# Sum of squares in a gated RMS norm: halves added before the product, one product in place of two

## What is computed

```python
y = (y_intra + y_inter).reshape(B, H, L, D).transpose(0, 2, 1, 3)
rms = jnp.sqrt(jnp.mean(jnp.square(y), axis=-1, keepdims=True) + RMS_EPS)
y = y / rms * gnorm_w
gate = (hidden_states @ Wg.T).reshape(B, L, H, D)
y = y * (gate * jax.nn.sigmoid(gate))
return y.reshape(B, L, H * D) @ Wo.T
```

## Time and profile before

| | us |
|---|---|
| median of 3 runs | 1121.64 |
| lowest, highest | 1119.6, 1122.24 |
| the profiled execution's own time | 1125.82 |
| its span in the trace (first to last instruction) | 1124.0 |
| PE busy in it | 1078.1 (96%) |
| DVE, ACT, POOL busy | 768.3, 550.6, 206.4 |

### The profile page before, as it was taken

How to read it: one execution, slowest core, us unless ns; L and a number is a source line. 1 busy time by engine, 2 the same in 40 slices (tenths; PEclk the granted TensorE clock), 3 DMA queues, 4 the chain that set the end, 5 groups by cost and what they waited for, 6 DMA issues and landing times. The chain is left out here.

```text
span 1124.0 us, 14213 instructions
## 1 busy us (share of the span) xinstructions
PE 1078.1 (96%) x4680; PEld 808.6 (72%) x4680; DVE 768.3 (68%) x1492; ACT 550.6 (49%) x1133; POOL 206.4 (18%) x131
## 2 busy tenths in 40 slices
PE   5869999999999999999999999999999969999898
PEld 1747777777777777777777777777776448888676
DVE  5777876877788678868877887778676785444411
ACT  2445555666555566555666555666555434222300
POOL 2412121211222121122111221211121530000000
PEclk8989999999999999999999999999999989999999
DMA  6111311220131013102201310131030431111011
GB/s 221 48 52 56 121 38 37 83 77 19 37 112 37 19 37 112 37 27 82 95 19 37 103 46 19 37 112 37 19 106 22 192 130 40 56 37 57 29 38 37
DMA packets 37464, 70.89 MB, mean 63 GB/s; under 512 B 2936, under 2 KB 19576, under 8 KB 35520
## 3 DMA queue, kind: packets, MB, share of 16 engines
q1 hardware_dynamic: 36720, 70.16, 19.3%
q10 hardware_dynamic: 720, 0.43, 0.1%
HBM read 68.33 MB, written 2.24 MB: 63 GB/s over the span
## 5 line engine op out<-in xcount | busy, mean ns | idle before, releaser
L1299 POOL TENSOR_TENSOR q_sin<-q_sin,cst 128x512 f32<-128x512 f32 x64 | 83.0, 1296 | 395.8 <-ACT q_sin L751 395.8
L1292 POOL TENSOR_TENSOR dec<-dec,future 128x1024 f32<-128x1024 f32 x31 | 80.3, 2591 | 273.8 <-ACT expg L770 273.8
L54 PE MATMUL ps_gt<-hT_hi,wg_hi 128*128 128x512 f32 x256 | 126.4, 494 | 3.6 <-DVE sg L986 3.6
L848 ACT ACTIVATE work<-ps_y 128x512 f32<-128x512 f32 x64 | 38.3, 598 | 186.1 <-PE ps_y L673 185.3
L54 PE MATMUL ps_q<-hT_hi,wq_hi 128*128 128x512 f32 x256 | 126.5, 494 | 2.8 <-DVE q_cos L966 2.3
L54 PE MATMUL ps_o<-wo_hi,z_hi 128*128 128x512 f32 x260 | 104.1, 400 | 2.4 <-DVE z_lo L49 2.4
L56 PE MATMUL ps_o<-wo_hi,z_lo 128*128 128x512 f32 x260 | 103.1, 396 | 0.0
L55 PE MATMUL ps_o<-wo_lo,z_hi 128*128 128x512 f32 x260 | 102.7, 395 | 0.0
L55 PE MATMUL ps_gt<-hT_lo,wg_hi 128*128 128x512 f32 x256 | 101.9, 398 | 0.0
L56 PE MATMUL ps_q<-hT_hi,wq_lo 128*128 128x512 f32 x256 | 101.9, 398 | 0.0
L56 PE MATMUL ps_gt<-hT_hi,wg_lo 128*128 128x512 f32 x256 | 101.8, 398 | 0.0
(11 more groups left out here) (239 smaller groups left out, 2537.9 us busy)
## 6 DMA issues: line engine op xcount, KB each, us to landing
dec<-gT_dram SPq DMA_DIRECT2D x32, 512.0 KB, 5.4
raw_q<-wq_in SPq DMA_DIRECT2D x32, 256.0 KB, 2.6
raw_g<-wg_in SPq DMA_DIRECT2D x32, 256.0 KB, 2.9
raw_o<-wo_in SPq DMA_DIRECT2D x8, 1024.0 KB, 7.0
raw_pair<-wkv_in SPq DMA_DIRECT2D x8, 512.0 KB, 4.6
raw_pair<-wgu_in SPq DMA_DIRECT2D x6, 512.0 KB, 3.3
raw_gu<-wgu_in SPq DMA_DIRECT2D x5, 512.0 KB, 3.3
qT<-wmod_in SPq DMA_DIRECT2D x2, 1024.0 KB, 7.0
```

What stands on the lines that cost most here:

```text
L54: pe.matmul(out, w_hi, x_hi, start=first, stop=False)
L848: nc.scalar.activation(sq, ps_y[:], ACT.Square).then_inc(sq_done, 1)
L1292: nc.gpsimd.tensor_tensor(cells, cells, future[:].unsqueeze(1).broadcast_to([P, GRP * CPB, CHUNK]), ALU.add).then_inc(mask_done, 1)
L1299: nc.gpsimd.tensor_tensor(q2, q2, sinT, ALU.mult).then_inc(qsin_done, 1)
```

## The change

`y^2` is a sum over 128 partitions, so the upper 64 can be added to the lower 64 first. ACT now writes the squares of partitions 0 to 63 into `sq[0:64]` and those of 64 to 127 into a new tile `sq_top`, both float32. DVE adds them into `sq_sum` (64 x 512). ACT rounds `sq_sum` into partitions 0 to 63 of `sq_parts` (`round_squares`, new), and DVE writes the rest into partitions 64 to 127 of it. One product of ones with `sq_parts` then sums high and low halves together. On PE the whole of `g_block` (12 products) stands ahead of it.

```diff
             def square_sum(g, t):
 
                 pe.wait_ge(sqhi_done, g * 8 + (t + 1))
-                nc.tensor.matmul(ps_ss[:], ones[:], sq_hi[:], start=True, stop=False)
                 pe.wait_ge(sqlo_done, g * 8 + (t + 1))
-                nc.tensor.matmul(ps_ss[:], ones[:], sq_lo[:], start=False, stop=True)\
+                nc.tensor.matmul(ps_ss[:], ones[:], sq_parts[:], start=True, stop=True)\
                     .then_inc(ss_ready, 1)
...
                 if project:
-                    g_block(g, t, 0, KT - 1)
+                    g_block(g, t, 0, KT)
                 square_sum(g, t)
-                if project:
-                    g_block(g, t, KT - 1, KT)
...
+            def round_squares(g, t):
+                act.wait_ge(sqsum_done, g * 8 + (t + 1))
+                nc.scalar.activation(sq_parts[0:64], sq_sum[:], ACT.Copy).then_inc(sqhi_done, 1)
...
-                nc.scalar.activation(sq, ps_y[:], ACT.Square).then_inc(sq_done, 1)
-                nc.scalar.activation(sq_hi[:], ps_y[:], ACT.Square).then_inc(sqhi_done, 1)
+                nc.scalar.activation(sq[0:64], ps_y[0:64], ACT.Square)
+                nc.scalar.activation(sq_top[:], ps_y[64:128], ACT.Square).then_inc(sq_done, 1)
...
                 if c == 1:
                     copy_kT(g, b)
+                round_squares(g, t)
                 decays(g, t + 1)
...
-                dve.wait_ge(sqhi_done, g * 8 + (t + 1))
-                split_lo(nc.vector, sq_lo[:], sq, sq_hi[:]).then_inc(sqlo_done, 1)
-                dve.wait_ge(sqlo_done, g * 8 + (t + 1))
+                dve.wait_ge(sq_done, g * 8 + (t + 1))
+                nc.vector.tensor_tensor(sq_sum[:], sq[0:64], sq_top[:], ALU.add).then_inc(sqsum_done, 1)
+                dve.wait_ge(sqsum_done, g * 8 + (t + 1))
                 dve.wait_ge(sg_done, g * 8 + (4 * half + 4))
                 nc.vector.tensor_tensor(z[:], ps_y[:].rearrange("p (h i) -> p h i", h=GRP),
                                         sg[:, half, :, rows_of(t)], ALU.mult).then_inc(zz_done, 1)
+                dve.wait_ge(sqhi_done, g * 8 + (t + 1))
+                split_lo(nc.vector, sq_parts[64:128], sq_sum[:], sq_parts[0:64]).then_inc(sqlo_done, 1)
```

More of the change, by code:

```diff
@@ L231, in block_attention @@
         sq = work[:].rearrange("p h i -> p (h i)")
-        sq_hi, sq_lo = sb("sq_hi", [P, HALF], F32R), sb("sq_lo", [P, HALF], F32R)
+        sq_parts = sb("sq_parts", [P, HALF], F32R)
+        sq_top, sq_sum = sb("sq_top", [P // 2, HALF]), sb("sq_sum", [P // 2, HALF])
+        win_lo = sb("win_lo", [P, KT, P], F32R)
         rms = sb("rms", [P, HALF])
@@ L249, in block_attention @@
         silu_c = sb("silu_c", [P, KT * B])
-        win, win_hi, win_lo = (w[:].rearrange("p (k h) -> p k h", k=KT) for w in (q_cos, sq_hi, sq_lo))
+        win, win_hi = (w[:].rearrange("p (k h) -> p k h", k=KT) for w in (q_cos, sq_parts))
         rows = cross[:, 1, 0:2 * H].rearrange("p (r h) -> p r h", r=2)
@@ L329, in block_attention @@
         sq_done = sem("sq_done")
+        sqsum_done = sem("sqsum_done")
         sqhi_done = sem("sqhi_done")
@@ L1108, in _ @@
                     dve.wait_ge(win_split, 1)
-                    split_lo(nc.vector, win_lo, win, win_hi).then_inc(win_split, 1)
+                    split_lo(nc.vector, win_lo[:], win, win_hi).then_inc(win_split, 1)
             dve.wait_ge(tables_loaded, 16)
```

## The result

The changed kernel takes 1176.12 us in the median of 4 runs (1174.0 to 1176.79), the kernel before 1121.94 (1119.6 to 1123.52). The ratio is 1.0475, 95% interval 1.0456 to 1.0493: slower by 54 us. The prediction was 1165, range 1146 to 1178: the direction and the mechanism held, and the size was 11 us short, a fifth of the loss. The result lies only 2 us under the top of the range.

A forecast was written before the change was run, and what follows sets the result against it. The prediction took PE, saturated in the loop, as the bound. A stall in every step, net of the removed product, gave +39 us and the tail +4: 1121.64 + 43 = 1165 us, range 1146 to 1178.

The forecast's parts named there:

- The bound: In the loop, PE limits the time: busy for all 750.00 us between 100 and 850 us.
- The other signs: PE's busy share falls about 6%; line 690 waits about 60 times, 40 to 50 us; DVE's sum takes 0.69 us.
- Part 1: On PE, one product of squares less saves 0.23 us a step, 14 us in 60 steps.
- Part 2: On PE, three gate products move ahead without added work, giving the chain from `ps_y` 2.62 us to make `sq_parts`.
- Part 3: Chain on ACT and DVE: low half late, PE idle 0.78 us, step +0.66 us net, +39 us in 60 steps.
- the rule that says so: On DVE, an instruction starting in another partition group waits for earlier ones: up to 0.05 us a step, 3 us in all.
- The restart: On PE after a wait, the next product comes 0.34 us later instead of 0.23, with 0.23 as low bound.
- the high end of the range: 0.70 us a step, 10 us in the tail and a few for the cover: 1177 us.
- Part 4: Work behind the waits: exponentials just fit and cost nothing; `z_lo` keeps 0.64 of 1.34 us of cover.
- Part 5: Tail, steps 4 to 7 of the last group without gate products in front: +4 us, bounds 1 and 10.
- the chain is hidden, whole or half: Two rivals on the chain to `sq_parts`: fully hidden, about 1112 us; half hidden, 1117 to 1124; chance 0.04 each.
- The third rival: Cover of `z_lo` at the out product or of the exponentials on ACT breaks too: 15 us more, 1180; chance 0.08.

The follow-up runs named there:

- the order of PE alone: Kernel before with the whole gate block moved ahead of its two products of squares, nothing else touched: 1123.74 us, ratio 1.0003.
- the changed kernel with one wait: Changed kernel without PE's wait for the high half ahead of the product of squares: 1170.09 us, ratio 1.0422 to the kernel before.
- The kernel with `z` behind: Changed kernel with `z` computed behind the low half on DVE instead of ahead of it: 1180.48 us, ratio 1.0501 to the kernel before.

## Why the prediction was right, and what it missed

- **The bound** was PE, without any slack in the loop, and the changed kernel shows 44 us of idle PE in the same stretch. Right. The other signs that were named are there too: PE waits at line 690 for the low half 64 times and 49.5 us in all.
- **Part 1, the product that goes: 14 us.** Right in size when it is tried alone with cover behind the gate block (13.2 us in the loop). In its old place it gave 5.
- **Part 2, the order costs nothing.** Right, 1.0003.
- **Part 3, the chain.** Up to the start of the rounding every entry is within 0.01 us of the trace: the squares 0.60 apart, half height no cheaper, the sum at 1.23. Then two terms were too small. The low half starts 0.04 later than I had it; `z` is in front of it, and it does not overlap `z`. I had the rule that says so and left it out of the sum. And the hand-over to PE was taken as 0.05 from the earlier trace rows, where the product has one wait; line 690 has two, and it took 0.14. The restart was 0.31, not 0.34. Together the step is 0.75 us longer (15.26 us the even one, 12.16 the odd one), not 0.65. In 60 steps that is 6 of the 11 us missed. It is also more than the 0.70 that the high end of the range allowed.
- **What the prediction did not look at: the end of the loop's pass.** In step 7 the next scores start 0.59 us behind the product, not 0.31:

```profile
299.50 0.46 PE L690 MATMUL ps_ss<-sq_parts,ones_r 128*128 128x512 f32 x1 [0.73 <-DVE sq_parts L49]
300.09 1.12 PE L662 MATMUL ps_s<-qT,kT 128*128 128x512 f32 x2
```

  Step 7 is 0.38 us longer by it than the other odd steps, in the six passes that another follows; the last is 0.13 longer; 2.5 us in all. The trace shows the loop's jump (line 391) in PE's sequencer between the two products:

```profile
L391 PEldq ALU_OP  x1: 32/32/32, 299.5 to 299.5; - x1
L391 PEldq COMPARE_BRANCH  x1: 213/213/213, 299.6 to 299.6; - x1
L391 PEldq FUSED_REGOPS  x1: 50/50/50, 299.9 to 299.9; - x1
```

  With the order of PE alone, two products of squares are the last of the pass as well, but PE does not stop in front of them. There the same jump (line 388) lies at 494.7 to 495.2, the scores start at 495.92 in full stride, and step 7 takes 11.43 us like the other odd steps. So here the jump costs nothing while PE still has products to work on, and is paid when it comes behind a wait.
- **Part 4, the cover.** Right. The logarithm starts 0.26 us behind the end of the exponentials (339.71 to 339.97), so they cost nothing, and in the loop PE never waits for `z_lo` (the one wait of 2.4 us behind the last step is in both traces): in odd steps it is ready 7.73 us after `ps_y`, and its reader starts at 8.36, 0.63 of cover against 0.64 predicted. The reader that was missing in this part, the out product's other operand `wo_lo`, does not bind in the changed kernel, since the stall in even steps moves PE back as well. It binds as soon as the stall is mended.
- **Part 5, the tail: +4.** It was +7.5, of which 0.75 belongs to the 60th step. Step 4 gave 0.85 against 0.7 predicted, step 5 gave 0.72 against 1.3, step 6 alone 3.3 against 1.3. (Step 5 was long before already, 14.88 us with the subtraction of 1.81 us; in the profiles of the five other kernels with that tail it takes 13.8 to 14.0, so that against them it is some 1.6 longer.) What comes behind the last `ps_y` is 1.9 longer, where 0.4 was predicted and the product comes 0.64 later; in the six profiles whose tail has no added halves this stretch lies between 223.4 and 226.3 us (226.3 changed), so the rest of it shows nothing. Step 6: its product starts at 941.60, 1.8 us later than before after `ps_y`, half a microsecond more than I had. The rest is the clock. PE had nothing to do from 939.3 to 941.6, and from 942.8 on the granted clock was at the lower of its two levels, 1.2 GHz. By stretch (first number of the pair behind the busy times is the clock), and two rows of the out product in it:

```profile
942.80:946.20 3.40, 3.40 (x10) 2.62 (x9) 1.46 (x5) 0.63 (x2) 0.00 (x0) 0.52 0.00 0
```

```profile
942.61 0.39 PE L54 MATMUL ps_o<-wo_hi,z_hi 128*128 128x512 f32 x1
...
943.60 0.63 PE L54 MATMUL ps_o<-wo_hi,z_hi 128*128 128x512 f32 x1
944.03 0.63 PE L55 MATMUL ps_o<-wo_lo,z_hi 128*128 128x512 f32 x1
```

  Products there are 0.43 apart instead of 0.23, and the seven that fell into it make some 1.4 us. In the profile of the changed kernel with one wait, which differs in the tail by that wait alone, PE stands idle just as long, but the clock stays at 1.00 and step 6 took 8.96 us and not 10.50. The kernel with `z` behind has the dip too. So that part is one that a run may have or not.
- **The rivals.** That the chain is hidden, whole or half, failed on the point named: half height buys nothing (0.685 us for 64 partitions of the sum). The third rival, a cover that breaks besides, is not what added the 11 us. That the measured time lies in the range owes something to luck: its high end was made of 10 us for the tail and a few for the cover, and what filled it was the step, the loop's jump and the clock.

What was mis-sized, in the prediction's own words, is "PE starts 0.05 later, as at 883.69", which took 0.14, and "the low half begins when the rounding is there", which took 0.04 more: 39 us for 60 steps, where 45 were measured. The loop's jump behind a wait, 2.5 us, stood at nothing.

## What to carry to other kernels

Before an instruction is taken from a saturated engine, look how early its operand is: what the product saves is lost where its operand comes later than that. Here 0.32 us of cover, and 0.46 more by the gate products that moved ahead, stood against a chain that became 1.56 us longer (1.84 to 3.40 us from `ps_y` to the low half). If the chain must be longer, move the product behind other work and list every reader of what comes later, also those that share a queue with it; then the gain may come out, here 5 us with 22 of the 60 steps changed, where the plain change lost 54. Halving the partitions of an elementwise instruction saved nothing here (0.685 us for the sum on 64 partitions, 0.69 for the subtraction on 128), so a sum across halves is paid in full.

## What the runs showed of the hardware that I had not expected

- A second wait on an instruction cost 0.07 to 0.09 us: 0.14 against 0.05 from DVE to PE, and 0.10 against 0.03 from ACT to DVE. In both cases the wait that is written last stands in the trace as an instruction of its own ahead of the other, and it was also the one that ended last. Where the wait that ends last is written first (`z` behind the sum: 337.87 to 337.91), the instruction of the other wait had run at 337.21, and there is no such delay. Swapping the two waits alone was not tried.
- After a wait of PE the next product starts 0.31 to 0.34 us later instead of 0.23, so each stall costs about 0.1 us beyond its length. A jump of the loop behind such a wait cost 0.38 us more here.
- In the loop, idle stretches of 0.74 us in every 12 to 15 us left the granted clock at 1.00.
